# Attention and conditional convolutions on one core: score banks, pool banks and P @ V visits regrouped

## The reference, cut to what matters

```python
# x: (16, 256, 32, 32); for each image b, in two stages
xn  = group_norm(x, 32 groups) * gn_w + gn_b
q, k, v = split(qkv_w @ xn + qkv_b)                # 4 heads of 64 channels, n = 1024 positions
attn = softmax(q.T @ k / 8)                        # per head, 1024 x 1024
x  = x + proj_w @ (v @ attn.T) + proj_b
rw = sigmoid(mean(x) @ router_w.T + router_b)      # 8 gates
w1, w2, w3 = sum_e rw[e] * experts[e]              # 1x1, 3x3 and 1x1 convolutions of this image
h  = relu(bn1(conv(x, w1)));  h = relu(bn2(conv(h, w2)))
x  = relu(bn3(conv(h, w3)) + x)
```

## Time and profile before

| | |
|---|---|
| median of 3 runs | 1908.56 us (1905.64 to 1909.35) |
| the profiled execution | 1908.05 us, its span 1906.3 us |
| mean granted clock of TensorE | 0.995 |
| TensorE busy | 1853.7 us, 97% |
| GpSimd busy | 1433.9 us, 75% |
| ScalarE busy | 1083.5 us, 57% |
| VectorE busy | 1041.8 us, 55% |
| chain that ended last | TensorE 87%, VectorE 5%, issue 3% |

### The profile page before, as it was taken

The page is one execution under the profiler, slowest core; times in us unless marked ns, Lnnn a source line. Parts: engine busy times, 40 slices in busy tenths (PEclk is TensorE's granted clock), DMA queues, the critical chain, the costliest instruction groups (busy, mean ns, idle before and its releaser), DMA issues.

```text
span 1906.3 us, 29566 instructions
## 1 busy us (share of the span) xinstructions
PE 1853.7 (97%) x8370; PEld 1065.4 (56%) x8370; DVE 1041.8 (55%) x1820; ACT 1083.5 (57%) x1501; POOL 1433.9 (75%) x827
## 2 busy tenths in 40 slices
PE   6899999999999999999999999999999999999988
PEld 5455556555555555555555565555555555555543
DVE  6656556464654646555464554646556465554625
ACT  5455646556565565656556575564655557465452
POOL 3677968778796886968779687786968779687582
PEclk9999999999999999999999999999999999999999
DMA  4022423324233233332324233242332323323233
...
DMA packets 96673, 166.72 MB, mean 87 GB/s; under 512 B 26112, under 2 KB 26880, under 8 KB 96640
## 3 DMA queue, kind: packets, MB, share of 16 engines
...
...
## 4 chain that ended last, share of the span: by engine, by line
PE 87%; DVE 5%; issue 3%; POOL 2%; ACT 2%; DMA 1%; DVEq 0%; SPq 0%; POOLq 0%; ACTq 0%
PE PV L807 23%; PE R L634 14%; PE S L789 12%; PE R L771 11%; PE S L792 10%; PE R L690 5%; PE R L729 3%; DVE mx L1024 3%; PE R L682 2%; PE R L737 2%; PE R L713 1%; POOL psum_p L606 1%; PE R L695 1%; DVE K L1045 1%; ACT K L908 1%
## 5 line engine op out<-in xcount | busy, mean ns | idle before, releaser
L606 POOL TENSOR_TENSOR psum_p<-psum_p,prob 128x1024 f32<-128x1024 f32 x382 | 911.0, 2385 | 306.4 <-ACT prob L893 287.4
L1024 DVE TENSOR_REDUCE mx<-R 128x1 f32<-128x512 f32 x1006 | 653.2, 683 | 584.6 <-PE R L771 577.6
L893 ACT ACTIVATE prob<-S 128x1024 f32<-128x1024 f32 x512 | 518.2, 1022 | 320.6 <-PE S L792 315.6
L807 PE MATMUL PV<-prob,V 128*64 128x512 f32 x2048 | 470.3, 601 | 0.0
L789 PE MATMUL S<-Q,K 128*128 128x512 f32 x1024 | 445.7, 435 | 2.5 <-ACT prob L893 2.5
L792 PE MATMUL S<-Q,K 128*128 128x512 f32 x1024 | 403.2, 394 | 2.4 <-DMA Q<-mrow 2.4
L771 PE MATMUL R<-K,Q 128*128 128x512 f32 x1006 | 336.9, 405 | 13.3 <-DVE mx L1024 7.8
L807 PEld LDWEIGHTS PV<-prob,V 128*64 128x64 f32 x2048 | 136.2, 137 | 255.7 <-issue 240.0
L789 PEld LDWEIGHTS S<-Q,K 128*128 128x128 f32 x1024 | 193.2, 189 | 131.7 <-issue 82.1
L771 PEld LDWEIGHTS R<-K,Q 128*128 128x128 f32 x1006 | 186.1, 188 | 94.5 <-DVE mx L1024 48.3
L792 PEld LDWEIGHTS S<-Q,K 128*128 128x128 f32 x1024 | 193.7, 189 | 47.1 <-issue 14.3
...
## 6 DMA issues: line engine op xcount, KB each, us to landing
ex<-in_experts_dram SPq DMA_DIRECT2D x122, 352.0 KB, 3.3
...
K<-K SPq DMA_DIRECT2D x128, 128.0 KB, 2.3
Q<-Q SPq DMA_DIRECT2D x128, 128.0 KB, 2.3
...
```

Source lines behind the costliest of these rows:

```text
L606: nc.gpsimd.tensor_tensor(acc, first_in, prob[:, s % PBUF, :, :], ALU.add).then_inc(add_done, 1)
L807: last = nc.tensor.matmul(PV[own(a), :], V[:, b // NH, kt, a * D:a * D + D], prob[:, s % PBUF, a, :], start=(kt == 0), stop=(kt == KT - 1))
L893: nc.scalar.activation(prob[:, s % PBUF, :, :], S[:, s % 2, :, :], ACT.Exp, scale=D ** -0.5).then_inc(exp_done, 1)
L1024: nc.vector.reduce_max(mx[:, b % 2, nh, m:m + 1], R[:, fill_bank(b, m, nh), :], AX.X).then_inc(max_read, 1)
```

## The change

The score tile is handled by halves: each has its own bank, its own `exp` and its own count in `s_done` and `exp_done`. S has three banks instead of four, and `S_BANKS` gives the 64 halves of an image in a ring of three (with one exchange in the middle, so that the next image begins anew with bank 0). R has four banks instead of three.

`BATCH` goes from 4 to 2: a visit to P @ V follows every second step, for two steps, so there are 16 per image. The jobs behind visits stand behind five of them, as before.

The job `row` and the identity go. VectorE now turns the block's maxima by four transposes of 32 x 32, and K2 holds -1 where it held 1. SyncE's transfers of the rows stand in `LOADS`. VectorE sums the two halves of the pooled image, so that `router` has two matmuls (four instructions) instead of four (eight). Ten `keep_busy` matmuls stand ahead of the first scores. All the lists of places, banks and works are new.

```diff
-BATCH = 4
+BATCH = 2
 TURNS = STEPS // BATCH
-PLACES = {2: [("proj", -1, 0)], 3: [("row", 0, 1)], 4: [("gna", 1, 0)], 6: [("proj", -1, 1)], 7: [("qk", 0, 7), ("gnb", 1, 0)],
-          8: [("proj", -1, 2)], 9: [("proj", -1, 3)], 10: [("router", -1, 0)], 11: [("row", 0, 2)], 13: [("qk", 1, 0)],
-          15: [("qk", 1, 1), ("qk", 1, 2)], 17: [("v", 1, 0)], 18: [("v", 1, 1)], 21: [("v", 1, 3)], 22: [("qk", 1, 3)],
-          24: [("v", 1, 4)], 25: [("v", 1, 5)], 26: [("v", 1, 6)], 27: [("row", 1, 0)], 28: [("v", 1, 7)], 29: [("qk", 1, 4)]}
-HALVES = {3: [("z", 0, 0)], 4: [("z", 0, 1), ("conv1", -1, 0)], 5: [("conv2a", -1, 0), ("conv2", -1, 0), ("z", 0, 2)],
-          6: [("conv3", -1, 0), ("conv3", -1, 1)], 7: [("conv3", -1, 2), ("conv3", -1, 3), ("z", 0, 3)]}
-BANK_OF = {"qk": (1, 1, 2, 1, 2, 2, 2, 0), "v": (0, 2, 0, 1, 0, 1, 1, 2), "row": (1, 2, 1, 1), "proj": (2, 0, 1, 1), "gna": (2,),
-           "gnb": (1,), "router": (1,), "conv1": (0,), "conv2": (2,), "z": (0, 2, 0, 1), "conv3": (1, 2, 2, 0)}
-FILL_BANKS = ((0, 1), (0, 1), (0, 1), (0, 1), (0, 1), (2, 0), (1, 2), (1, 2), (2, 0), (0, 2), (0, 2), (0, 2), (2, 1), (2, 0), (0, 2), (0, 2),
-              (2, 0), (2, 1), (0, 1), (2, 1), (1, 2), (2, 0), (0, 2), (0, 2), (1, 2), (2, 0), (0, 2), (0, 2), (1, 0), (0, 1), (0, 1), (0, 1))
-EARLY = {0: [("qk", 0, 6)], 19: [("row", 0, 3), ("v", 1, 2)], 31: [("qk", 1, 5)]}
+PLACES = {0: [("qk", 0, 6)], 2: [("proj", -1, 0)], 5: [("gna", 1, 0)], 7: [("proj", -1, 1), ("qk", 0, 7), ("gnb", 1, 0)],
+          8: [("proj", -1, 2)], 9: [("proj", -1, 3)], 10: [("router", -1, 0)], 15: [("qk", 1, 2)], 16: [("v", 1, 0)],
+          20: [("v", 1, 1), ("v", 1, 2)], 21: [("v", 1, 3)], 24: [("v", 1, 4)], 25: [("v", 1, 5), ("v", 1, 6)], 28: [("v", 1, 7)],
+          29: [("qk", 1, 4)], 30: [("qk", 1, 5)]}
+HALVES = {5: [("z", 0, 0)], 9: [("z", 0, 1), ("conv1", -1, 0)], 11: [("conv2a", -1, 0), ("conv2", -1, 0), ("z", 0, 2)],
+          13: [("conv3", -1, 0), ("conv3", -1, 1)], 15: [("conv3", -1, 2), ("conv3", -1, 3), ("z", 0, 3)]}
+BANK_OF = {"qk": [0, 1, 3, 3, 2, 3, 0, 3], "v": [0, 2, 1, 2, 0, 2, 0, 0], "proj": [3, 1, 1, 0], "gna": [2], "gnb": [0],
+           "router": [0], "conv1": [3], "conv2": [0], "z": [3, 0, 2, 2], "conv3": [2, 3, 1, 0]}
+FILL_BANKS = ((3, 1), (3, 2), (1, 0), (0, 1), (0, 3), (1, 0), (1, 3), (0, 2), (0, 3), (3, 2), (2, 1), (0, 3), (3, 1), (0, 3), (2, 3), (2, 0),
+              (2, 1), (2, 1), (2, 0), (2, 0), (1, 0), (3, 0), (1, 3), (2, 1), (3, 2), (1, 3), (2, 3), (2, 1), (2, 3), (1, 3), (0, 1), (0, 2))
+S_BANKS = (0, 1, 2) * 10 + (0, 1, 0, 2) + (0, 1, 2) * 10
+EARLY = {14: [("qk", 1, 0)], 15: [("qk", 1, 1)], 19: [("qk", 1, 3)]}
 PROLOGUE = [("gna", 0, 0), ("gnb", 0, 0)] + [("qk", 0, f) for f in range(4)] + [("v", 0, f) for f in range(8)] + [("bias", 0, 0), ("qk", 0, 4), ("qk", 0, 5)]
 EPILOGUE = ([("proj", 0, f) for f in range(4)] + [("router", 0, 0), ("conv1", 0, 0),
@@ -99,32 +102,29 @@
 DIRECT = (30, 31)
-WORK = {1: [("low", 0, 12)], 3: [("low", 0, 13)], 5: [("proj", -1, 0), ("stats", 1, 0)],
-        7: [("stats", 1, 1), ("recip", -1, 3), ("row", 0, 1)], 8: [("gna", 1, 0)], 13: [("proj", -1, 1)],
-        15: [("gnb", 1, 0), ("low", 0, 14), ("low", 0, 15)], 17: [("proj", -1, 2)], 19: [("proj", -1, 3)], 21: [("router", -1, 0)],
-        22: [("gates", -1, 0), ("row", 0, 2)], 27: [("low", 1, 0)], 29: [("low", 1, 1)],
-        31: [("low", 1, 2), ("low", 1, 3), ("low", 1, 4), ("low", 1, 5)], 37: [("row", 0, 3)], 38: [("recip", 0, 0)],
-        46: [("low", 1, 6), ("low", 1, 7)], 52: [("recip", 0, 1)], 53: [("recip", 0, 2), ("row", 1, 0)],
-        55: [("conv3", -1, 0), ("conv3", -1, 1)], 59: [("low", 1, 8), ("low", 1, 9)], 61: [("low", 1, 10)], 62: [("low", 1, 11)],
-        63: [("conv3", -1, 2), ("conv3", -1, 3)]}
-ACT_WORK = {7: [("normal", 1, 0)], 9: [("normal", 1, 1)], 10: [("product", -1, 0), ("product", -1, 1)],
-            13: [("product", -1, 2), ("product", -1, 3)], 15: [("product", -1, 4), ("product", -1, 5)],
-            18: [("product", -1, 6), ("product", -1, 7)]}
-POOL_WORK = {7: [("deviations", 1, 0)], 8: [("affine", 1, 0), ("norm", -1, 3)],
-             11: [("split", 1, 0), ("gates", -1, 0), ("split", 1, 1), ("mix", -1, 1)], 13: [("mix", -1, 2), ("mix", -1, 3)],
-             16: [("mix", -1, 4), ("mix", -1, 5)], 18: [("mix", -1, 6), ("mix", -1, 7)], 23: [("norm", 0, 0)], 28: [("norm", 0, 1)],
-             31: [("norm", 0, 2)]}
-LOADS = {3: [("v1", 0, 0)], 14: [("xin", 2, 0)], 16: [("xin", 2, 1)], 19: [("xin", 2, 2), ("xin", 2, 3)], 22: [("h", -1, 0)]}
-def build(nc, x, vecs, router_b, wqkv, wproj, wrouter, experts, neg_eye, group_avg, out):
+WORK = {1: [("low", 0, 12), ("low", 0, 13)], 6: [("stats", 1, 0), ("recip", -1, 3)], 7: [("proj", -1, 0), ("stats", 1, 1)],
+        11: [("gna", 1, 0)], 15: [("proj", -1, 1), ("gnb", 1, 0), ("low", 0, 14), ("low", 0, 15)], 17: [("proj", -1, 2)],
+        19: [("proj", -1, 3), ("router", -1, 0)], 20: [("gates", -1, 0)], 28: [("low", 1, 0), ("low", 1, 1)],
+        30: [("low", 1, 2), ("low", 1, 3)], 31: [("low", 1, 4), ("low", 1, 5)], 35: [("recip", 0, 0)],
+        37: [("low", 1, 6), ("low", 1, 7)], 51: [("recip", 0, 1)], 54: [("recip", 0, 2)], 55: [("conv3", -1, 0), ("conv3", -1, 1)],
+        60: [("low", 1, 8), ("low", 1, 9)], 62: [("low", 1, 10)], 63: [("conv3", -1, 2), ("conv3", -1, 3), ("low", 1, 11)]}
+ACT_WORK = {7: [("normal", 1, 0)], 9: [("normal", 1, 1)], 10: [("product", -1, 0), ("product", -1, 1)], 13: [("product", -1, 2)],
+            14: [("product", -1, 3)], 15: [("product", -1, 4), ("product", -1, 5)], 18: [("product", -1, 6)], 19: [("product", -1, 7)]}
+POOL_WORK = {6: [("norm", -1, 3), ("deviations", 1, 0)], 8: [("affine", 1, 0)], 9: [("split", 1, 0)],
+             11: [("gates", -1, 0), ("split", 1, 1), ("mix", -1, 1)], 13: [("mix", -1, 2), ("mix", -1, 3)], 14: [("mix", -1, 4)],
+             15: [("mix", -1, 5)], 17: [("mix", -1, 6), ("mix", -1, 7)], 24: [("norm", 0, 0)], 29: [("norm", 0, 1), ("norm", 0, 2)]}
+LOADS = {2: [("row", 0, 1)], 9: [("row", 0, 2)], 13: [("v1", 0, 0)], 16: [("row", 0, 3)], 18: [("h", -1, 0)], 19: [("xin", 2, 0)],
+         23: [("xin", 2, 1)], 26: [("row", 1, 0)], 27: [("xin", 2, 2)], 30: [("xin", 2, 3)]}
...
-        S = pb("S", [P, 2, 2, HALF])
+        S = pb("S", [P, len(set(S_BANKS)), HALF])
         PV = pb("PV", [P, HALF])
-        R = pb("R", [P, 3, HALF])
+        R = pb("R", [P, 4, HALF])
...
+        def s_bank(s, a):
+            return S[:, S_BANKS[2 * s + a], :]
+        def scores_before(s, a):
+            n = 2 * s + a
+            return next(d for d in range(1, 2 * STEPS) if S_BANKS[(n - d) % (2 * STEPS)] == S_BANKS[n])
...
-                sp.wait_ge(read["row"], BLOCKS * i + b + 1)
+                sp.wait_ge(max_turned, BLOCKS * i + b + 1)
                 for a in range(2):
                     r = 64 - 64 * a
-                    sp.dma_start(Q2[r:r + 1, 2 * p + a, px(hf)].bitcast(F32),
-                                 mrow[QT * a:QT * a + QT, :].bitcast(F32)).then_inc(rows_loaded, 16)
+                    sp.dma_start(Q2[r:r + 1, 2 * p + a, px(hf)].bitcast(F32), mxt[QT * a:QT * a + QT, :]).then_inc(rows_loaded, 16)
...
-                        pool.wait_ge(exp_done, STEPS * i + s + 1)
+                        pool.wait_ge(exp_done, 2 * (STEPS * i + s + 1))
...
-                elif kind == "row":
-                    pe.wait_ge(max_ready, BLOCKS * i + f + 1)
-                    last = nc.tensor.matmul(bank[0:2 * QT, 0:P], mx1[:, :], negeye[:, :], start=True, stop=True)
...
-                    pe.wait_ge(read["proj"], 4 * i + 4)
+                    pe.wait_ge(pooled, i + 1)
                     for c in range(CC):
-                        for hf in range(NH):
-                            last = nc.tensor.matmul(bank[:, 0:E], pool4[:, c, hf:hf + 1].to_broadcast([P, P]), wr[:, c, :],
-                                                    start=(c + hf == 0), stop=(c + hf == CC + NH - 2))
+                        last = nc.tensor.matmul(bank[:, 0:E], pool2[:, c:c + 1].to_broadcast([P, P]), wr[:, c, :], start=(c == 0), stop=(c == CC - 1))
...
             def scores(i, s):
                 b, kt = s // KT, s % KT
                 p, hf = b // NH, b % NH
-                wait(pe, exp_done, STEPS * i + s - 1)
                 for a in range(2):
                     h = 2 * p + a
-                    nc.tensor.matmul(S[:, s % 2, a, :], K1[:, h, kt * P:kt * P + P], Q1[:, h, px(hf)], start=True, stop=False)
+                    wait(pe, exp_done, 2 * (STEPS * i + s) + a + 1 - scores_before(s, a))
+                    if isinstance(i, int) and (i, s, a) == (0, 1, 0):
+                        pe.wait_ge(read["qk"], 6)
+                    nc.tensor.matmul(s_bank(s, a), K1[:, h, kt * P:kt * P + P], Q1[:, h, px(hf)], start=True, stop=False)
                     if kt == 0 and a == 0:
                         pe.wait_ge(rows_loaded, 32 * (BLOCKS * i + b + 1))
```

(42 more changed lines are left out.)

38 lines of the change are left out of this document (20 added, 18 removed).

## The result

The changed kernel takes **1949.41 us** (median of 4 runs, 1946.81 to 1951.2) against 1907.89 us before (4 runs, 1905.64 to 1909.35): a ratio of 1.0218, 95% interval 1.0200 to 1.0235. It is slower by 2%, where 1890 us, faster by 1%, was forecast. The profiled execution took 1950.74 us, its span is 1949.0.

A forecast was written before the change was run, and what follows sets the result against it. TensorE was taken to bound the kernel, 97% busy. The profiled 1908.05 us, less 9 for the first image, plus 15 x (112.47 + 2.4 - 115.48), gave 1890 us; range 1864 to 1924.

The forecast's parts named there:

- The price of a visit: On TensorE, each visit to P @ V costs 0.36 to 0.37 us whatever it contains; eight more add 2.96 us per image.
- The floor: One image without any stall on TensorE would last 112.47 us, against 115.48 before.
- row job, router and group norm: TensorE work saved per image: row job gone, -1.47 us; four fewer router instructions, -0.4; group-norm job against a visit, -0.1.
- conv1's 1.3: End of step 19: conv1 waits for the last mixed kernel through ScalarE and GpSimd, 1.3 us of stall.
- step 21's 0.7: Behind conv1, ScalarE writes the padded image before the next half exp: 0.6 us of stall and 0.1 for starting again.
- the half exp of step 17: Steps 15 to 17: qk jobs, products and the copy of o precede this half exp on ScalarE, 0.4 us of stall.
- A fourth bank: With visits every second step, it removes TensorE's waits for VectorE's maxima, within 4.0 us of stalls per image.
- Even 4 x 0.28 is hidden: VectorE's four transposes a block, at up to 0.28 us each, cost nothing: their rows are needed over 10 us later.
- the 2.4 us an image for stalls: Stalls expected to come back on TensorE per image, bounds 0.5 and 5.4 us.
- the score ring's rival: Eight qk jobs on ScalarE each delay the second half score 0.4 us: stall 5.4 us, 1935 us; chance 0.18.
- The -9 us: First image: VectorE waits in the extra fills and the half-clock first visit go, gaining 9 us, bounds 3 and 11.
- Copies 114.9 us apart: Sign: conv2's result copies, one per image, should be 114.9 us apart after the change.

The follow-up runs named there:

- e1: The kernel before with one part of the change alone, sixteen visits to P @ V per image instead of eight: 1963.89 us, ratio 1.0306.
- e3: The changed kernel with VectorE's low parts 6 and 7 moved from step 18 to behind the maxima of step 19: 1947.22 us, ratio 1.0211.
- e2: The changed kernel with eight visits per image again (every fourth step), all else as changed: 1855.24 us, ratio 0.9736.
- e9: The changed kernel with block 2's final maximum and four transposes moved behind the maxima of step 11: 1937.23 us, ratio 1.0162.
- e7: The changed kernel with eight visits, and low part 11 ahead of conv3's last two reads on VectorE: 1846.91 us, ratio 0.9677.
- e11: e7 with block 2's final maximum and four transposes moved behind the maxima of step 11: 1848.1 us, ratio 0.9694.
- e10: The changed kernel with low parts 6, 7 and 11, product 7, and block 2's final maximum and transposes reordered: 1916.29 us, ratio 1.0056.
- e4: The changed kernel with VectorE's router read moved from half step 19 to 21 and the gates from 20 to 22: 1965.55 us, ratio 1.0316.

## Why the prediction was wrong

**What held.** The price of a visit: a fill in front of one takes 0.32 us, the eight products 1.87, the score behind 0.34, as the working had it, and e1's period has the 2.96 us an image. The floor held: 118.40 - 5.8 = 112.6 against 112.47, so row job, router and group norm are priced rightly together. Of the stalls named as coming back, conv1's 1.3 is in e3 (1.33 idle), step 21's 0.7 measured 0.55, and the half exp of step 17, 0.4, measured 0.3.

**What failed** is one sentence: "A fourth bank, and a visit of 2.05 us (1.70 of products, 0.36 of change) after every second step, take these away: in each turn VectorE has 4.8 us, against 2.4 of maxima and mostly no more than 1.5 of other work." The sum for a turn is right, since VectorE is busy for only 56% of the span. But it is no rate that decides. A job's bank asks that certain maxima be read by the moment at which TensorE reaches it, and VectorE's order may hold work, and waits, ahead of them. What covers that is the visit just in front of the job, and the change halves it: 3.59 us with sixteen instructions, 1.87 with eight. So the same edit that costs eight transitions also takes 1.7 us of slack from each job behind a visit. At step 19 chain and cover are 3.76 against 2.43; with the long visit 3.75 against 4.14 (e2). The fourth bank and the visits were counted together as a help; the visits are, on balance, the opposite of one.

The same fault is in the sentence "Even 4 x 0.28 is hidden". The transposes take 0.84 us for four, 0.21 each, inside the bounds. The working asked when their row is needed, over 10 us later, and not what stands behind them on VectorE: the maxima of step 11, which the row sums want 2.4 us after the first fill and had after 3.1. At sixteen visits the final maximum and the transposes there cost 0.9 us an image, 12 us of result (e9).

In the sum the term is the 2.4 us an image for stalls, which measured 5.8. Those 3.4 to 3.5 us over the steady images and the last are some 50 us of the 61 by which the profiled execution missed. Step 19, the clearest case, is hardly part of them: its 1.46 us stand where the forecast had 1.3 for conv1, and hide it (e3). The rest of what was not forecast, 3.5 us, is of two kinds. Steps 11, 9, 4 and 5 lose 1.9, all of it gone with eight visits (e2). Steps 0, 15 and 28 lose 1.6, which eight visits leave as it is: there an order of VectorE's list or a late read is enough by itself, and at step 0 another order took the stall away (e7). So the fourth bank too was counted on for more than it gives. The bound of 5.4 for it, the score ring's rival at 1935 us, was nearer in size but not in kind: scores wait for exp in steps 9, 17 and 21 and lose 1.3 us in all, of which only step 9's 0.44 was not forecast. The waits for maxima and bank reads of steps 0, 4, 5, 11, 15, 19 and 28 lose 4.5.

**The first image.** The -9 us came out as nothing, the other 9 us of the miss. With eight visits the same kernel gains 9.2 there, so the argument from the banks was right; in the changed kernel the eight more visits (3.0), the visit at the lower clock at 79.50 (1.6) and further waits use it up. The first visit did run at full clock, but the first fills still waited 0.94 us for VectorE.

**Sizes of the theories.** The dose is measured in one kernel: 8, 16 and 32 visits give 1855, 1949 and 2066 us. Of the 94 us between the first two, half is the price of the transitions and half are stalls that come with the short visits. That cover is what is lost is shown at step 19 by e2's trace and at step 11 by e9 against e11. For the stalls of steps 4, 5, 9 and 17, which also go with eight visits, it is only argued. The rival, single wrong places, is worth a part: four mends took the period from 118.40 to 116.17 (e10), some 33 us, while one alone gave 12 us (e9), 2 us (e3) or lost 16 (e4). The two shares overlap: the stall of step 11 goes by either, a longer visit or a shorter list. No run at sixteen visits was faster than the kernel before. Whether a full new order of the lists would be is open; it was not tried.

**By the signs it named.** Copies 114.9 us apart: 118.4, wrong. Visits of eight in 1.85 us: 1.87, right. "PE or PEld fill <- DVE" should nearly go: wrong, L773 still waits for VectorE in steps 0, 4 and 5. conv1 over 1 us for mix: hidden behind another wait, seen in e3. Step 21 waits for exp: right. First visit at full clock: right. None of its three signs of being wrong came: scores wait for exp in three steps only, a visit costs what was said, and no matmul of the row sums waits for GpSimd. It had no sign for row sums that wait for VectorE.
